# Four-head attention scores with a running maximum, and routing with wide 0/1 counts, in one kernel

## The reference, cut to what matters

```python
# per layer; H = 16 heads of 32, B = 8
q = split_heads(layernorm(x) @ w_q + b_q);  k, v = the same of ctx (8, 722, 512)
scores = einsum('bhqd,bhkd->bhqk', q, k) / sqrt(32)
scores = where(mask == 0, -1e9, scores)              # layer 0 only
attn = softmax(scores, axis=-1)
x = x + tanh(g_xattn) * (merge(attn @ v) @ w_out + b_out)
h = layernorm(x)
p = softmax(h @ gate_w)                              # 64 experts, top 8 (layer 0); 8 experts, top 2 (layer 1)
shared = silu_or_gelu_mlp(h)                         # all tokens
routed = sum over chosen experts of weight * expert(h)   # layer 0: at most 256 tokens an expert
x = x + tanh(g_ffn) * (shared + routed)
```

## Time and profile before

| | us |
|---|---|
| three runs | 2495.83, 2503.39, 2504.03; median 2503.39 |
| the profiled execution, its own time | 2507.09 |
| its span from first to last instruction | 2505.3 |
| mean granted TensorE clock over the span | 0.929 of full speed |
| TensorE busy | 2253.1 |
| VectorE busy | 1216.8 |
| ScalarE busy | 936.2 |
| GpSimd busy | 535.5 |

### The profile page before, as it was taken

One profiled execution on the slowest core, in us unless ns is written; L12 is line 12 of the kernel. 1 busy time (PEld: TensorE's weight loads), 2 busy tenths in 40 slices (PEclk: granted clock), 3 DMA queues, 4 the chain that ended last, 5 costly groups with the idle time before them and its releaser, 6 DMA issues. The chain is left out here.

```text
span 2505.3 us, 39432 instructions
## 1 busy us (share of the span) xinstructions
PE 2253.1 (90%) x13564; PEld 1581.1 (63%) x13565; DVE 1216.8 (49%) x2072; ACT 936.2 (37%) x1523; POOL 535.5 (21%) x574
## 2 busy tenths in 40 slices
PE   6899999987893899999848999999869997999995
PEld 4777777765861444444427777777659535777773
DVE  3466666654722222222264666666533014777776
ACT  2355555543110111111112555555433104656663
POOL 0000000001375455445400000000012301232321
PEclk9899999985896899999968999999858998999997
DMA  4300000003000999999630100000030005756652
GB/s 155 133 30 30 30 30 30 1 1 131 1 1 22 334 319 344 317 335 286 155 147 29 37 32 25 25 25 1 1 132 1 34 0 220 279 216 213 244 186 65
DMA packets 64805, 287.89 MB, mean 115 GB/s; under 512 B 11740, under 2 KB 12142, under 8 KB 45354
## 3 DMA queue, kind: packets, MB, share of 16 engines
q1 hardware_dynamic: 42842, 246.40, 26.2%
q0 software_dynamic: 21840, 39.69, 7.4%
HBM read 257.85 MB, written 33.96 MB: 116 GB/s over the span
## 5 line engine op out<-in xcount | busy, mean ns | idle before, releaser
L582 ACT ACTIVATE probs<-ps,stat 100x722 f32<-100x722 f32 x256 | 219.3, 862 | 152.4 <-DVE stat L519 76.0
L1214 PE MATMUL pgu<-ring,xT 128*128 x560 | 267.5, 601 | 6.5 <-issue 2.4
L434 PE MATMUL pt<-ident,probs 100*128 100x100 f32 x1536 | 194.3, 266 | 50.2 <-ACT pTs L570 49.2
L570 ACT ACTIVATE pTs<-pt 128x600 f32<-128x600 f32 x256 | 171.9, 671 | 114.2 <-PE pt L434 108.3
L434 PEld LDWEIGHTS pt<-ident,probs 100*128 100x128 f32 x1536 | 158.5, 149 | 86.2 <-DVE probs L507 45.7
L1214 PEld LDWEIGHTS pgu<-ring,xT 128*128 128x128 f32 x560 | 100.2, 192 | 114.0 <-issue 113.6
L507 DVE TENSOR_SCALAR probs<-probs,stat 100x722 f32<-100x722 f32 x256 | 157.6, 616 | 9.1
L1571 DVE TENSOR_TENSOR ws_low<-w,ws_high 128x2048 fp32r<-128x2048 f32 x63 | 142.9, 2291 | 24.1 <-ACT ws_high L1502 24.1
L1260 ACT ACTIVATE sg<-pgu 128x256 f32<-128x256 f32 x70 | 26.9, 384 | 313.2 <-PE pgu L1214 313.2
L1228 PE MATMUL pd<-ring,hT 128*128 x280 | 132.7, 596 | 1.7 <-issue 0.8
L519 DVE CUSTOM_DVE_ANT_0 ps<-ps,madd 100x722 f32<-100x722 f32 x128 | 114.1, 933 | 36.0 <-PE ps L425 36.0
(11 more groups left out here) (252 smaller groups left out, 5084.5 us busy)
## 6 DMA issues: line engine op xcount, KB each, us to landing
ring<-in_l_ew SPq DMA_DIRECT2D x64, 1536.0 KB, 8.8
w<-in_l_ew SPq DMA_DIRECT2D x64, 1024.0 KB, 8.0
xnT<-in_ctxT SPq DMA_DIRECT2D x14, 1444.0 KB, 7.0
wu<-in_l_up SPq DMA_DIRECT2D x2, 4096.0 KB, 12.6
b<-in_l_eb SPq DMA_DIRECT2D x8, 1024.0 KB, 4.7
moe_sum<-zrow SPq DMA_DIRECT2D x3, 2048.0 KB, 13.4
moe<-moe_sum SPq DMA_DIRECT2D x24, 200.0 KB
wd<-in_l_down SPq DMA_DIRECT2D x2, 2048.0 KB, 11.6
```

What stands on the lines that cost most here:

```text
L434: last = pe.transpose(pt[:, kc // 3, (kc % 3) * S:(kc % 3 + 1) * S], probs[s % 4][:, kc * P:(kc + 1) * P], ident[0:S, 0:S])
L570: act.activation(pTs[:, g % 2, s % HPC, :, :].rearrange("k (a c) q -> k a (c q)", a=2), pt[:, :, 0:3 * S], ACT.Copy).then_inc(t_out, 1)
L582: act.activation(probs[s % 4][:, 0:SK], scores_of(s), ACT.Exp, bias=stat[:, s, 1:2], scale=-1.0 if masked else 1.0, accum_out=stat[:, s, 2 ...
L1214: last = pe.matmul(pgu[p][:, :], xT[p][:, c, :], wgu[c], start=c == 0, stop=c == DC - 1)
```

## The change

In the attention:

- `SEG` becomes 0 to 362 and 362 to 722. The unit of work is one segment of four heads (a "half"): `scores` makes 3 parts x 4 heads in four groups of 32 rows, into four PSUM tiles `ps` of one bank each.
- Each half has its own maxima and exponents. When both halves of a group of four are there, their maxima are compared (`segments_apart`), ScalarE makes e to the difference (`shares`), and VectorE makes from shares and sums one factor for each head and segment (`factors`, four small operations, two more in `segments_apart`). `normalised` multiplies each segment by its factor.
- `probs` has eight tiles without padding; the last chunk of keys has 82 rows in transposes and values.
- A body has eight halves, 4 to 11; 8 to 11 are the next batch's first four. Transposes of a group come two halves after its scores. The prologue weaves the 14 pieces with four halves.
- The output bias, times the gate, is added to `x` by GpSimd during the query projection, so the residual reads PSUM alone. The zeroing of `moe_sums` and `xn_rows` moves to that block too. The mask is loaded into `madd` directly.

In the routing:

- `ones`, `before` and `chosen` get rounded copies, and the counts are float32r: one product for tile 0, seven with `ones` whose columns are all later tiles (`broadcast_to`), one with `before` for tiles 1 to 7, 8 for the totals.
- Constant casts of VectorE (`iota_e`, `behind`, `entry`, `lvl`, `tile_n`) come before the logits.
- The scatters take `entry` and `slot_at` directly, without copies, in one written-out loop and on one semaphore.
- `slot_indices` goes; load, transposes and copies of the table stand at the end of `dense_and_route`. The tables are allocated for each layer.

```diff
-SEG = ((0, 512), (512, SK))
+SEG = ((0, 362), (362, SK))
...
+                    sp.dma_start(bo[:, :], b_o.broadcast_to([S, D])).then_inc(bo_in, 16)
...
+                @block.gpsimd
+                def _(pool):
...
+                    pool.tensor_scalar(bo[:, :], bo[:, :], env.gate[0:S, layer:layer + 1], None, ALU.mult)\
+                        .then_inc(bo_scaled, 1)
+                    pool.wait_ge(bo_scaled, 1)
+                    for t in range(B):
+                        pool.tensor_tensor(x[:, t, :], x[:, t, :], bo[:, :], ALU.add).then_inc(x_biased, 1)
...
-        probs = [sb(f"probs{n}", [S, KC * P]) for n in range(4)]
+        probs = [sb(f"probs{n}", [S, SK]) for n in range(2 * HPC)]
-        ps = [cx.enter_context(nc.psum_tensor(env.name(f"ps{n}"), [P, 1024], F32)) for n in range(2)]
+        ps = [cx.enter_context(nc.psum_tensor(env.name(f"ps{n}"), [P, 512], F32)) for n in range(HPC)]
...
+        BESIDE = {4: (("k", 0, 0), ("k", 0, 1)), 5: (("k", 1, 0), ("k", 1, 1)), 6: (("k", 2, 0), ("k", 2, 1)),
+                  7: (("v", 0), ("v", 1)), 8: (("k", 3, 0), ("k", 3, 1)), 9: (("v", 2), ("v", 3)),
+                  10: (("v", 4), ("v", 5)), 11: ()}
...
+                def scores(b, p, g, seg, first=False):
+                    if g == 0 and seg == 0:
+                        pe.wait_ge(q_ready, b * 2 + 2)
+                    pe.wait_ge(piece_out, b * NPIECE + (PIECES.index(("k", g, seg)) + 1))
                     if not first:
-                        pe.wait_ge(exp_done, b * H + 2 * i)
-                    for k0, k1 in SEG:
-                        for x, y in PARTS:
-                            for s in (2 * i, 2 * i + 1):
...
+                        pe.wait_ge(exp_done, b * (2 * H) + (g * 2 + seg) * HPC)
+                    k0, k1 = SEG[seg]
+                    for x, y in PARTS:
+                        for j in range(HPC):
+                            rows = slice(j * DH, (j + 1) * DH)
+                            last = pe.matmul(ps[j][0:S, 0:k1 - k0], qb[p][x][rows, g, :], kT[y][rows, g, k0:k1],
+                                             start=(x, y) == PARTS[0], stop=(x, y) == PARTS[-1])
...
+                    for h in HALVES:
+                        if h < NHALF or left:
+                            scores(*at_half(b, p, h))
...
+                        if h % 2 == 0:
+                            weighted_values(b, p, h // 2 - 2, left)
+                        if pieces:
+                            piece(pieces[0])
                         if turn:
+                            transposed(tb, tg, 2 * late)
+                        if pieces:
+                            piece(pieces[1])
+                        if h == HALVES[-1]:
+                            outputs(b, left)
                         if turn:
+                            transposed(tb, tg, 2 * late + 1)
...
+                        if h < NHALF or left:
+                            maxima(bb, bp, g, seg)
+                            if seg == 1:
+                                segments_apart(bb, g)
+                        if seg == 0 and (h < NHALF + 2 or left):
+                            normalised(tg, 2)
+                            normalised(tg, 3)
+                        for what in pieces[:1]:
+                            piece_rest(dve, what, b + 1, 1 - p)
+                        if seg == 1 and (h < NHALF or left):
+                            factors(bb, g)
+                        if h == HALVES[-1]:
+                            residual()
+                        if seg == 1 and (h < NHALF or left):
+                            normalised(g, 0)
+                            normalised(g, 1)
+                        for what in pieces[1:]:
+                            piece_rest(dve, what, b + 1, 1 - p)
+                        if left == 2:
+                            for part in {10: (0, 1), 11: (2,)}.get(h, ()):
+                                split_low(dve, b + 2, part)
...
+                        if h < NHALF + 3 or left:
+                            turned(lb, lg, 2 * l_late + 1)
...
+                            exponents(bb, g, seg, (0, 1))
+                        if h % 2 == 0:
+                            heads_out(b, h // 2 - 2)
+                        elif pieces:
+                            piece_high(act, pieces[0], b + 1)
+                        if active:
+                            exponents(bb, g, seg, (2, 3))
+                            if seg == 1:
+                                shares(bb, g)
+                        if pieces and h % 2 == 0:
+                            piece_high(act, pieces[0], b + 1)
+                        if h < NHALF + 2 or left:
+                            turned(tb, tg, 2 * late)
...
-                        for t in range(B):
-                            for j in range(t + 1):
-                                pe.matmul(ppos[:, t * E:(t + 1) * E], (before if j == t else ones)[:, :],
-                                          chosen[:, j, :], start=j == 0, stop=j == t)
+                        pe.matmul(ppos[:, 0:E], before_r[:, :], chosen_r[:, 0, :], start=True, stop=True)
+                        for j in range(B - 1):
+                            pe.matmul(ppos[:, (j + 1) * E:B * E].rearrange("s (t e) -> s t e", e=E), ones_r[:, :],
+                                      chosen_r[:, j:j + 1, :].broadcast_to([S, B - 1 - j, E]), start=j == 0,
+                                      stop=False, skip_group_check=True)
+                        pe.matmul(ppos[:, E:B * E], before_r[:, :],
+                                  chosen_r[:, 1:B, :].rearrange("s t e -> s (t e)"), start=False, stop=True,
+                                  skip_group_check=True)
...
+                for t in range(B):
                     for k in range(K):
                         pool.indirect_dma_start(
-                            out=env.slot_table[:, :], in_=entry_now[p][:, k, :], in_offset=None,
-                            out_offset=bass.IndirectOffsetOnAxis(ap=slot_now[p][:, k:k + 1], axis=0))\
-                            .then_inc(scattered[p], 16)
+                            out=env.slot_table[:, :], in_=entry[:, t, k, :], in_offset=None,
+                            out_offset=bass.IndirectOffsetOnAxis(ap=slot_at[:, t, k:k + 1], axis=0))\
+                            .then_inc(scattered, 16)
...
+                sp.wait_ge(scattered, B * K * 16)
+                sp.dma_start(table[:, :, :], env.slot_table[0:slots, :].rearrange("(r n) a -> r n a", n=P))\
+                    .then_inc(table_in, 16)
...
-                slot_indices(nc, env, SLOTS0 // P)
```

More of the change, by code:

```diff
@@ new lines, in outputs, with first_piece @@
+                def outputs(b, more):
+                    pe.wait_ge(ao_ready, b * NG + NG)
+                    if more:
+                        pe.wait_ge(piece_out, b * NPIECE + (NPIECE + PIECES.index(("v", 4)) + 1))
+                    for c in range(DC):
+                        last = pe.matmul(pp[0:S, :], aoT[:, c, :], wo[:, c, :], start=c == 0, stop=c == DC - 1)
+                    last.then_inc(o_mm, 1)
+                def first_piece(*what):
+                    make_piece(pe, what, 0, True)
@@ new lines, in _, with residual @@
+                maxima(0, 0, 1, 1)
+                segments_apart(0, 1)
+                first_piece("k", 3, 1)
+                split_low(dve, 1, 0)
+                first_piece("v", 2)
+                factors(0, 1)
+                normalised(1, 0)
+                normalised(1, 1)
+                first_piece("v", 3)
+                split_low(dve, 1, 1)
+                first_piece("v", 4)
+                first_piece("v", 5)
+                split_low(dve, 1, 2)
+                def body(b, p, left):
+                    def residual():
+                        dve.wait_ge(o_mm, b + 1)
+                        xb = x[:, b:b + 1, :] if isinstance(b, int) else x[:, bass.ds(b, 1), :]
+                        xb = xb.rearrange("q a n -> q (a n)")
+                        dve.scalar_tensor_tensor(out=xb, in0=pp[0:S, :], scalar=env.gate[0:S, layer:layer + 1], in1=xb,
+                                                 op0=ALU.mult, op1=ALU.add).then_inc(res_done, 1)
+                    for h in HALVES:
+                        bb, bp, g, seg = at_half(b, p, h)
+                        _, _, tg, late = at_half(b, p, h - 2)
+                        pieces = BESIDE[h] if left else ()
+                        if h < NHALF or left:
[19 more added lines that the diff above has]
+                                split_low(dve, b + 2, part)
@@ new lines, in exponents @@
+                def exponents(b, g, seg, heads, first=False):
+                    k0, k1 = SEG[seg]
+                    for j in heads:
+                        if not first:
+                            act.wait_ge(t_mm, b * H + (g * HPC + j - 7))
+                        act.wait_ge(max_ready, b * (2 * H) + ((g * 2 + seg) * HPC + j + 1))
```

(9 more changed lines are left out.)

530 lines of the change are left out of this document (249 added, 281 removed).

## The result

| | median of the runs | range | profiled execution: own time, span, clock |
|---|---|---|---|
| before | 2503.71 us (4 runs) | 2495.83 to 2507.68 | 2507.1, 2505.3 |
| after | 2432.69 us (4 runs) | 2427.57 to 2439.83 | 2436.6, 2434.9, 0.939 |

The ratio is 0.9722, with a 95% interval of 0.9685 to 0.976: faster, by 71 us. The prediction was 2383 with a range of 2340 to 2440. The range holds the time by 7 us, the likeliest value is 50 us too low, and the narrower 2355 to 2412, which was given a chance of 0.60, does not hold it. Both profiled executions are some 4 us above their medians, so the traces can be laid side by side. One execution of `s_sp`, a variant further down, took 10489 us where its other three took 2408 to 2413; it is left out, and nothing here explains it.

A forecast was written before the change was run, and what follows sets the result against it. The prediction took TensorE, busy 90% of the span, as the bound. Attention 80, layer 0's routing 29 and layer 1's 11 made 120 us off 2507.1: 2387, or 2383 as the median, range 2340 to 2440.

The forecast's parts named there:

- moved work: Attention: zeroing DMAs moved into the projection block and the output bias given to GpSimd; 2 us lost.
- layer 0's routing: Layer 0, up to the experts' first load: 16 us from an earlier scatter start, 7 from shorter scatters, 6 at the end; 29.
- the floor of 57.6: Full attention body in layer 0: 61.5 us less 3.9 us for scores of four heads at once.
- waits of 0.3 and 1.8 us: Attention body: second transpose waits for a copy in half 5 (0.3 us); work piles up in half 11 (1.8 us).
- some 3.6 us earlier: Layer 0's routing: casts leave the path before `chosen`, so TensorE starts counting about 3.6 us sooner.
- The 12 us for the counts: Layer 0's counts: 17 products instead of two-pass ones, 2.5 us with weight loads or 4 at low clock; 12 us gained.
- The scores: Attention scores, four heads running as two do: 0.165 us a group, 0.66 a half, 3.9 us less a batch.
- The prediction's other estimate: Scores by the skill's figure of 3.07 for four tiles: 0.22 us a group, 1.3 us a batch more than the sum.
- Two after two: Rival in the attention scores: four row groups do not run together, 62 us back, 2445 us; chance 0.08.
- The written order stalls: Rival in the attention: each half waits 0.35 us more, bodies 61.3 us, 40 us back, 2423 us; chance 0.14.
- everything overlaps: Rival in the attention: bodies at 56.8 us, prologues 5 and tails 4 shorter, 2339 us; chance 0.12.
- Slower: Rival in the attention: VectorE's queue becomes the bound as halves don't cost half, bodies 68 us, 2523 us; chance 0.04.

The follow-up runs named there:

- s_sp: Changed kernel, but SyncE waits for a semaphore GpSimd raises once after all scatters have landed; 2410.4 us (three runs), 0.9647 of before.
- turn_early: Changed kernel with TensorE's loop turn behind the output products, and layer 0's last eight routing products and two splits on VectorE; 2379.1 us, 0.9513 of before.
- early: Changed kernel with the last eight products and two splits of layer 0's routing moved from GpSimd to VectorE; 2393.5 us, 0.9578 of before.
- t_turn: Changed kernel with TensorE's loop over the batches turned behind an even batch's output products, ahead of its last transposes; 2392.6 us, 0.9572 of before.
- the repeats: The changed kernel itself, unaltered, run two more times beside the variants; 2411.5 us (0.9642 of before) and 2408.7 us (0.9633).
- the three rotated kernels: Changed kernel with TensorE's turn behind the output products: alone (2392.6 us), with SyncE on a once-raised semaphore (2396.9), with GpSimd's late routing work on VectorE (2379.1).

## Why the prediction was right, and where its sum was not

The time lies in the range and most steps hold: the gain comes where it was forecast, and the attention and the routing each give it alone. The range was needed, though. The sum was 120 us and the traces give 70.5. Two things, neither of them in the prediction, make up 42 of the 50 missing, 19.3 at the loop's turns and 22.7 in the late increments:

| step | forecast | measured | why |
|---|---|---|---|
| layer 0, six full bodies | 18 | 7.1 | two turns 9.3, bodies at 58.8 for 58.5 and the last |
| layer 1, six full bodies | 17 | 2.8 | two turns 10.0, bodies at 58.6 for 57.8 |
| prologue and first body, layer 0 | 8 | 4.8 | prologue 2.2 longer, body 7.0 shorter |
| the same, layer 1 | 11 | 8.8 | prologue 4.1, body 4.7 |
| last batches | 28 | 31.5 | 45.3 and 45.0 for 47 |
| moved work | -2 | -1.7 | |
| layer 0's routing | 29 | 2.7 | increments 22.7, casts 2.4 |
| layer 1's routing | 11 | 14.0 | |
| the rest | 0 | 0.5 | |

1. **"I expect 58.5 us a body in layer 0."** 58.8, and 57.6 for the last: right between turns. Its own terms did not give it: the floor of 57.6 with waits of 0.3 and 1.8 us is 59.7. Measured, TensorE is busy for 56.8 us and stands for 1.8, of which 1.08 is the wait in half 11. The step that failed is that the prediction costed the move of the output products, from behind the last transposes to ahead of them, at nothing. They were the cover of TensorE's turn. Four turns cost 19 us in the trace; covering them gave 14 us of medians (`turn_early` beside `early`) and 16 to 19 (`t_turn` beside the repeats).
2. **"TensorE's own work ends at 756 then, still before the scatters at 775, so the latter decide."** True in the ten later traces with the changed routing, and false in the first. There the experts' first load went out 26 us later than the scatters alone would have set (748.7 + 6.1).
3. **The scatters.** 86.6 forecast, 87.2 in the repeats; 6 us to the experts' first load forecast, 6.1 measured. Their start came 13.3 us earlier instead of 16: the term "some 3.6 us earlier" for `chosen` was 1.2, since `iota_e` and `top_f` waited for GpSimd's splits. The prediction had let 0.7 come back. The casts moved ahead of the logits took 6.9 us, 2.1 of them `iota_e`'s wait, where VectorE had stood for 4.6, so 2.3 came back. With `top_f` free (`turn_early`) the term was 3.6 even so. The 12 us for the counts took them at 2.5, though the sentence ahead of it gives 4 at the low clock; they took 3.6 at a clock of 0.50, 11.1 less than before.
4. **The scores.** The second and third group of four are 0.16 us apart, forecast 0.165. The term was mis-sized all the same: the first group takes 0.25 and the end is bare, so the scores have 6.6 us of a body where they had 9.35. That is 2.8 less, not 3.9. The prediction's other estimate, 0.22 us a group and 1.3 us more a batch, would have given 2.6 and was nearer. In layer 1 a body is 58.6, not 57.8: TensorE is busy for 56.8 us of it and stands for 1.7, as in layer 0, so the missing mask read-out gained nothing.
5. **VectorE and ScalarE.** 43.8 and 36.6 us a body, forecast 46 to 48 and about 39; maxima 0.56 (0.55), exponents 0.57 (0.43 to 0.62), normalising 0.41 (0.36).
6. **The rivals.** Two after two is excluded by the groups' starts. "The written order stalls" gave 2423, near the first runs, but by another mechanism: a body without a turn has waits of 1.8 us in all. The rival "everything overlaps" was priced too low: bodies at 56.8 give 7 x 1.7 + 7 x 1.0 = 19, not 26, so 2346. "Slower" would have needed bodies of 67 us.

## What to carry to other kernels

When a loop's last instructions are reordered, ask what is issued but not done at its turn: here 3.5 us of products hid a turn of TensorE and 0.7 us of transposes did not, and each engine's loop may be rotated by itself, with no change in the order of the work. When an engine is the bound of a stage through what it starts (scatters behind weight splits), look at when its input is ready: 14 us stood between the slots and the first scatter, and VectorE did the splits in half the time. And when one trace shows a wait that no dependence explains, run the same kernel again before building a theory; 23 us of this one vanished.

## What the runs showed of the hardware

- A turn of TensorE's loop without cover shows as a wait of 2.9 to 3.7 us, in all 36 cases of nine traces, and in the changed kernel's first trace as 4.3 to 5.5 us of a body with the low clock behind it. Behind the output products (3.5 us) it shows in none of the twelve turns of the three rotated kernels, though one body of `turn_early`, behind such a turn, is 4 us longer. That a fetch of instructions takes the time is not shown; a shorter loop was not tried.
- In one trace TensorE's semaphore increments arrived up to 40 us late beside 64 scatters issued without a pause, while VectorE's own arrived at once. Eight later traces with the same unbroken scatters show none. The cause is open.
- A cast of 64 columns by VectorE waited out a GpSimd instruction of 2.4 us. The same cast took 0.20 us when it met none, so a few microseconds before `chosen` depend on how the two queues fall.
- GpSimd issues a scatter of 100 rows every 1.29 to 1.30 us by the median, copies or not, and 1.22 us of VectorE replace 2.40 of GpSimd for a split of 1,024 columns.
